# Softmax-weighted rows of a graph attention layer: the fold on VectorE replaced by sums on TensorE, with the numerators in PSUM

## What is computed

```python
feat = einsum('ni,rhid->rnhd', layernorm(x), conv)          # per edge type
el, er = sum(feat[type, src] * attn_l[type]), sum(feat[type, dst] * attn_r[type])
e = leaky_relu(el + er, 0.2)                                 # per edge and head
ex = exp(e - segment_max(e, dst)[dst])
h = segment_sum(ex / segment_sum(ex)[dst] * feat[type, src], dst) + h_bias
x = x + h
x = x + sum_e cw[:, e] * (gelu(layernorm(x) @ W1[e] + b1[e]) @ W2[e] + b2[e])   # cw: two largest of softmax
```

## Time and profile before

| | |
|---|---|
| device time, median of 3 runs | 2616.04 us (2614.4 to 2618.78) |
| span of the profiled execution | 2256.0 us |
| busy: PE, PEld | 1390.8, 1112.0 us |
| busy: DVE, ACT, POOL | 1210.3, 643.8, 1504.5 us |
| mean granted TensorE clock | 0.81 |
| L873 gathers | 1014, mean 1277 ns |
| L1020 multiplies, L1025 adds | 256.1 us (136), 246.2 us (106) |
| L1452 sums | 480 records, 112.1 us |

### The profile page before, as it was taken

One profiled execution on the slowest core, in us unless ns is written; L12 is line 12 of the kernel. 1 busy time (PEld: TensorE's weight loads), 2 busy tenths in 40 slices (PEclk: granted clock), 3 DMA queues, 4 the chain that ended last, 5 costly groups with the idle time before them and its releaser, 6 DMA issues.

```text
span 2256.0 us, 26567 instructions
## 1 busy us (share of the span) xinstructions
PE 1390.8 (62%) x7174; PEld 1112.0 (49%) x7174; DVE 1210.3 (54%) x2282; ACT 643.8 (29%) x2351; POOL 1504.5 (67%) x1213
## 2 busy tenths in 40 slices
PE   2637994016877766676766676656666455465456
PEld 1313441006767665666656565555565354465344
DVE  5413004146767656655656565665666454567462
ACT  3212331013443333333333232332333321223121
POOL 1604113388888888878888888888888887888530
PEclk9878997557999888888887878788888777786677
DMA  5462333743333333333333333333333333323210
GB/s 152 155 161 75 128 134 136 208 123 88 86 83 81 90 88 90 88 90 87 87 92 82 90 85 86 84 85 87 86 86 84 92 89 97 85 80 82 67 37 3
DMA packets 113692, 214.93 MB, mean 95 GB/s; under 512 B 58478, under 2 KB 70357, under 8 KB 109510
## 3 DMA queue, kind: packets, MB, share of 16 engines
q0 software_dynamic: 57936, 153.93, 25.8%
q1 hardware_dynamic: 38688, 25.68, 4.3%
q10 hardware_dynamic: 16892, 33.82, 4.0%
HBM read 172.86 MB, written 44.87 MB: 97 GB/s over the span
## 4 chain that ended last, share of the span: by engine, by line
POOL 56%; issue 17%; PE 3%; POOLq 2%; DVE 2%; ACT 0%; DMA 0%; DVEq 0%; ACTq 0%; SPq 0%
POOL rows L873 52%; PE y_ps L1436 1%; POOL node_row L890 1%; POOL out_dram L881 1%; PE hid_ps L1422 1%; POOL xrows L873 1%; POOLq L886 1%; POOLq L921 1%; POOLq L792 0%; DVE xrows L1084 0%; DVE xrows L1088 0%; DMA xrows<-table,idx_x 0%; ACT hT L1332 0%; POOLq L909 0%; DVE xo L1177 0%
## 5 line engine op out<-in xcount | busy, mean ns | idle before, releaser
L873 POOL DMA_INDIRECT rows<-table,idx_st x1014 | 1294.8, 1277 | 309.0 <-issue 308.7
L1436 PE MATMUL y_ps<-w,hT 128*128 128x256 f32 (+1 forms) x1920 | 526.6, 432 | 530.5 <-ACT hT L1332 514.4
L1436 PEld LDWEIGHTS y_ps<-w,hT 128*128 128x128 f32 (+1 forms) x1920 | 401.3, 216 | 624.3 <-ACT hT L1332 545.6
L1422 PE MATMUL hid_ps<-zT,w 128*128 128x128 f32 (+1 forms) x3840 | 486.8, 287 | 0.0
L1422 PEld LDWEIGHTS hid_ps<-zT,w 128*128 128x128 f32 x3840 | 472.9, 202 | 17.5 <-ACT hT L1332 11.2
L1332 ACT ACTIVATE hT<-hid_ps,b1t 128x128 f32<-128x128 f32 (+1 forms) x960 | 268.6, 370 | 251.7 <-PE hid_ps L1422 249.4
L1025 DVE TENSOR_TENSOR rows<-rows 128x2080 f32<-128x2080 f32 x106 | 246.2, 2322 | 20.4 <-ACT rows L1342 14.6
L1020 DVE TENSOR_TENSOR rows<-rows,ex 128x2080 f32<-128x2080 f32 (+1 forms) x136 | 256.1, 1902 | 1.6
L983 DVE TENSOR_TENSOR score<-score,rows 128x160 f32<-128x160 f32 x30 | 9.7, 325 | 457.5 <-SPq L838 395.9
L586 PE MATMUL feat_ps<-wc,xnT 128*125 128x512 f32 x480 | 230.7, 627 | 37.2 <-ACT xnT L519 25.1
L1311 ACT ACTIVATE th<-e_diff 128x160 f32<-128x160 f32 x30 | 10.1, 336 | 735.9 <-DVE e_diff L1001 735.9
(11 more groups left out here) (172 smaller groups left out, 974.5 us busy)
## 6 DMA issues: line engine op xcount, KB each, us to landing
table<-stage ACTq DMA_DIRECT2D x30, 1031.2 KB
rows<-table,idx_st POOLq DMA_INDIRECT x1014, 2.8
w<-in_L_ffn_W_dram SPq DMA_DIRECT2D x16, 512.0 KB, 14.3
blocks<-edge_row SPq DMA_DIRECT2D x1, 4351.5 KB, 54.2
x_all<-in_x_dram SPq DMA_DIRECT2D x3, 1250.0 KB
node_tab<-x_all SPq DMA_DIRECT2D x3, 1250.0 KB
wc<-_L_gnn_conv_weights_dram ACTq DMA_DIRECT2D x16, 128.0 KB, 6.7
attnb<-in_L_gnn_attn_l_dram SPq DMA_DIRECT2D x1, 1024.0 KB, 10.8
```

The lines of the kernel that those rows point to most:

```text
L873: q.indirect_dma_start(buf[:, k, :], None, table, bass.IndirectOffsetOnAxis(idx[:, col + k:col + k + 1], 0)).then_inc(landed, 16)
L1422: last = t.matmul(hid_ps[e % 2][:, m * P:m * P + n], w1[:, e, k, m * P:(m + 1) * P], zT[:, k, 0:n], start=(k == 0), stop=(k == KD - 1))
L1436: last = t.matmul(y_ps[p % 2][0:n, (e % 2) * D:(e % 2 + 1) * D], hT[e % 2][:, k, 0:n], w2[:, e, k, :], start=(k == 0), stop=(k == KH - 1))
```

## The change

The numerators are written a second time, into a PSUM bank `dve_ps` that only VectorE uses (`ex_ps`), and VectorE's multiplies read them there; `er9` moves to the same bank. ScalarE still reads them from SBUF. VectorE multiplies slots 0 to 20 (8 and then 13 in one instruction) and, where the degree is over 32, 32 to 39; ScalarE has slots 21 to 31 (44 activations in parts of 16, 16 and 12 where there were 12, 8 and 8). All folds are gone. TensorE adds all slots, 32 or 40, through the identity into `agg_ps`: slots 0 to 20 when VectorE is done (`weighed`), the last 8 under an If on a register that it loads from SBUF, and 21 to 31 when ScalarE is done. It frees the four slot groups one by one for GpSimd (`freed`), which now takes them in the order 0, 1, 2, 3.

```diff
-    BY_ACT = 7
+    ACT_LO, ACT_HI = 21, 32
-    er9 = [sb(f"er9{i}", [P, H, R1]) for i in range(2)]
+    agg_ps, dve_ps = bank("agg_ps"), bank("dve_ps")
+    ex_ps = dve_ps[:, 0:H * NS].rearrange("p (h k) -> p h k", h=H)
+    er9 = [dve_ps[:, H * (NS + i * R1):H * (NS + (i + 1) * R1)].rearrange("p (h r) -> p h r", h=H) for i in range(2)]
...
-            for n, s in enumerate((1, 3, 2, 0)):
+            for s in range(PAIRED):
                 if not isinstance(w, int) or w >= 2:
-                    if s:
-                        pool.wait_ge(folded, (w - 2) * 3 + (n + 1))
-                    else:
-                        pool.wait_ge(agg_ok, w - 1)
+                    pool.wait_ge(freed, (w - 2) * PAIRED + (s + 1))
...
             st.did(v.tensor_scalar(ex[:], rden[:], 2.0, -1.0, ALU.mult, ALU.add))
+            st.did(v.tensor_scalar(ex_ps, rden[:], 2.0, -1.0, ALU.mult, ALU.add))
...
-        def weighted(par, s, skip=0):
-            lo, hi = s * SLOTS + skip, (s + 1) * SLOTS
+        def weighted(par, lo, hi):
             r = rows[par][:, lo:hi, 0:AGG].rearrange("p k (h c) -> p k h c", h=H)
-            return v.tensor_tensor(r, r, bc(ex[:, :, lo:hi].rearrange("p h k -> p k h"), 3, HC), ALU.mult)
+            return v.tensor_tensor(r, r, bc(ex_ps[:, :, lo:hi].rearrange("p h k -> p k h"), 3, HC), ALU.mult)
...
-            st.did(weighted(par, 0))
+            st.did(weighted(par, 0, SLOTS))
...
-            st.did(weighted(par, 1))
+            st.did(weighted(par, SLOTS, ACT_LO))
...
             with dve.If(degree > PAIRED * SLOTS):
-                weighted(par, PAIRED)
+                weighted(par, PAIRED * SLOTS, NS)
                 dve.drain()
-                fold(par, 0, PAIRED)
-                dve.drain()
-            fold(par, 0, 1).then_inc(folded, 1)
+            st.wait()
+            dve.sem_inc(weighed, 1)
             for _ in gate:
                 pass
-            st.did(weighted(par, 2))
-            st.did(weighted(par, 3, BY_ACT))
-            st.wait()
-            dve.wait_ge(act_weighed, w + 1)
-            fold(par, 2, 3).then_inc(folded, 1)
             between()
-            dve.wait_ge(folded, w * 3 + 2)
-            fold(par, 0, 2).then_inc(folded, 1)
...
-            dve.wait_ge(agg_ok, w + 1)
+            dve.wait_ge(freed, (w + 1) * PAIRED)
...
-                weigh(w, par, 0, 3)
+                weigh(w, par, 21, 25)
                 gelu(u, 2)
-                weigh(w, par, 3, 5)
+                weigh(w, par, 25, 29)
                 gelu(u, 3)
-                weigh(w, par, 5, BY_ACT)
+                weigh(w, par, 29, ACT_HI)
...
-            pe.wait_ge(folded, w * 3 + 3)
-            for k in range(SLOTS):
-                last = t.matmul(agg_ps[:, 0:AGG], ident[:], rows[par][:, k, 0:AGG], start=(k == 0),
-                                stop=(k == SLOTS - 1))
-            last.then_inc(agg_ok, 1)
+            def add(k, start=False, stop=False):
+                return t.matmul(agg_ps[:, 0:AGG], ident[:], rows[par][:, k, 0:AGG], start=start, stop=stop)
+
+            degree = pe.value_load(nb_row[0:1, bass.ds(w * 2 + 1, 1)], min_val=0, max_val=E)
+            after(pe, acc_ok, w)
+            pe.wait_ge(weighed, w + 1)
+            for k in range(ACT_LO):
+                last = add(k, start=(k == 0))
+                if k % SLOTS == SLOTS - 1:
+                    last.then_inc(freed, 1)
+            with pe.If(degree > PAIRED * SLOTS):
+                for k in range(PAIRED * SLOTS, NS):
+                    add(k)
+            pe.wait_ge(act_weighed, w + 1)
+            for k in range(ACT_LO, ACT_HI):
+                last = add(k, stop=(k == ACT_HI - 1))
+                if k % SLOTS == SLOTS - 1:
+                    last.then_inc(freed, 1)
```

More of the change, by code:

```diff
@@ L642, in phase2 @@
     assert PAIRED == 4 and STATIC == 5 and W % 2 == 0
-    N_FRONT, N_EX, N_BEGIN, N_POST, N_GATE, N_MIX = 6, 6, 5, 16, 11, 1 + NE
+    N_FRONT, N_EX, N_BEGIN, N_POST, N_GATE, N_MIX = 6, 5, 5, 16, 11, 1 + NE
     N_XFRONT, N_XEX, N_CHUNK = 7, 7, 25
@@ L735, in phase2 @@
     act_weighed = sem("act_weighed")
-    folded = sem("folded")
-    agg_ok = sem("agg_ok")
+    weighed = sem("weighed")
+    freed = sem("freed")
     acc_ok = sem("acc_ok")
@@ L864, in _ @@
         q = nc.gpsimd
-        for i in range(2):
-            q.memset(er9[i][:], MASKED).then_inc(const_ok, 1)
         bt = Batches(pool, "pool")
@@ L977, in scores @@
             st.wait()
-            st.did(v.tensor_tensor(eh, bc(er9[par][:], 1, n), bc(hot, 2, H), ALU.mult))
+            st.did(v.tensor_tensor(eh, bc(er9[par], 1, n), bc(hot, 2, H), ALU.mult))
             st.wait()
@@ L1012, in exps @@
             st.did(v.tensor_scalar(ex[:], rden[:], 2.0, -1.0, ALU.mult, ALU.add))
+            st.did(v.tensor_scalar(ex_ps, rden[:], 2.0, -1.0, ALU.mult, ALU.add))
             st.wait()
             return st
-        def weighted(par, s, skip=0):
-            lo, hi = s * SLOTS + skip, (s + 1) * SLOTS
+        def weighted(par, lo, hi):
             r = rows[par][:, lo:hi, 0:AGG].rearrange("p k (h c) -> p k h c", h=H)
-            return v.tensor_tensor(r, r, bc(ex[:, :, lo:hi].rearrange("p h k -> p k h"), 3, HC), ALU.mult)
-        def fold(par, s, t):
-            a, b = (rows[par][:, i * SLOTS:(i + 1) * SLOTS, 0:AGG] for i in (s, t))
-            return v.tensor_tensor(a, a, b, ALU.add)
+            return v.tensor_tensor(r, r, bc(ex_ps[:, :, lo:hi].rearrange("p h k -> p k h"), 3, HC), ALU.mult)
         def weigh_all(w, par, st, gate, between):
-            st.did(weighted(par, 0))
+            st.did(weighted(par, 0, SLOTS))
             for _ in range(2):
                 next(gate, None)
-            st.did(weighted(par, 1))
+            st.did(weighted(par, SLOTS, ACT_LO))
             degree = dve.value_load(nb_row[0:1, bass.ds(w * 2 + 1, 1)], min_val=0, max_val=E)
@@ L1036, in weigh_all @@
                 next(gate, None)
+            with dve.If(degree > PAIRED * SLOTS):
+                weighted(par, PAIRED * SLOTS, NS)
+                dve.drain()
             st.wait()
-            alone(dve, dve_passed)
-            with dve.If(degree > PAIRED * SLOTS):
-                weighted(par, PAIRED)
-                dve.drain()
-                fold(par, 0, PAIRED)
-                dve.drain()
-            fold(par, 0, 1).then_inc(folded, 1)
+            dve.sem_inc(weighed, 1)
             for _ in gate:
                 pass
-            st.did(weighted(par, 2))
-            st.did(weighted(par, 3, BY_ACT))
-            st.wait()
-            dve.wait_ge(act_weighed, w + 1)
-            fold(par, 2, 3).then_inc(folded, 1)
             between()
-            dve.wait_ge(folded, w * 3 + 2)
-            fold(par, 0, 2).then_inc(folded, 1)
-            assert st.n == N_EX
+            assert st.n == N_EX, st.n
         def take(w):
-            dve.wait_ge(agg_ok, w + 1)
+            dve.wait_ge(freed, (w + 1) * PAIRED)
             v.tensor_copy(acc[:], agg_ps[:, 0:AGG].rearrange("p (h c) -> p h c", h=H)).then_inc(acc_ok, 1)
@@ L1267, in _ @@
         dve.sem_inc(cleared, 1)
+        for i in range(2):
+            v.memset(er9[i], MASKED).then_inc(const_ok, 1)
         dve.wait_ge(const_ok, 2)
@@ L1335, in weigh @@
         def weigh(w, par, lo, hi):
-            if lo == 0:
+            if lo == ACT_LO:
                 act.wait_ge(ex_step, w * N_EX + 2)
-            for k in range((PAIRED - 1) * SLOTS + lo, (PAIRED - 1) * SLOTS + hi):
+            for k in range(lo, hi):
                 for h in range(H):
@@ L1342, in weigh @@
                     last = a.activation(r, r, ACT.Copy, scale=ex[:, h, k:k + 1])
-            if hi == BY_ACT:
+            if hi == ACT_HI:
                 last.then_inc(act_weighed, 1)
@@ L1366, in window @@
             else:
-                weigh(w, par, 0, BY_ACT)
+                weigh(w, par, ACT_LO, ACT_HI)
             nb, g = bt.enter(w)
```

2 lines of the change are left out of this document (1 added, 1 removed).

## The result

The changed kernel takes 3117.75 us (3098.07 to 3126.99), before 2615.6 in the same comparison: a ratio of 1.190, 95% interval 1.186 to 1.195. It is 19% slower, where I had forecast 3% faster.

The account below looks back on a forecast made before the run. GpSimd's gathers, stalled by VectorE, were taken as the bound, moving to TensorE. Savings of 155 us less 78 for clock and queue gave net -77: 2616 to 2539 us, range 2455 to 2605.

Parts of the forecast that it names:

- the median of 2616.04 lies 360.0 above it, and I leave that part as it is: Starting point of the sum: profiled span 2256.0 us, with the 360.0 us up to the median carried over unchanged.
- The bound moves to TensorE: TensorE's round, 48.7 us for 32 slots and 52.4 for 40, bounds almost every window instead of GpSimd.
- GpSimd's waits: Gathers for the window after next start 3.7 us into TensorE's sums, taking slot groups as they are freed.
- Covered.: Gathers end after 43.3 us (28) or 58.4 (40), before they are wanted at 63.4 or 70.8.
- The stalls go: GpSimd's gathers beside VectorE's two-SBUF-input instructions lose their stalls, 11 to 12 us a window; mean near 0.95 us.
- ScalarE's part: Sixteen more activations put off gelu 3 by 1.92 us; TensorE waits 2.56 there, its first piece grows to 26.7.
- The clock: TensorE's clock falls after the 2.56 us wait in two of three windows: 4.0 us each, 2.7 a window.
- The queue: Register load, If and added waits in TensorE's queue cost 0.3 us a window.
- The rival for slower: TensorE's register load and If drain its queue and lower the clock: 9.6 us a window, 2711 us; chance 0.14.
- stalls stay: Rival: VectorE instructions with a PSUM input still stall GpSimd's gathers; +39, 2578 us; chance 0.09.

Follow-up runs that it names:

- the kernels in which gathers and multiplies do meet: Changed kernel with eleven memsets a gather, 2387.8 us (1.054); kernel before with PSUM numerators, one drain a window, three memsets a gather, 2254.77 us (0.997).
- the run with 1.70 us beside the folds and 0.95 beside the multiplies: Kernel before with multiplies reading numerators in PSUM, folds kept in SBUF, one drain a window and three memsets a gather: 2254.77 us, ratio 0.997.
- its control on the kernel before: Kernel before with one drain a window alone, no memsets: 2597.38 us, ratio 0.992.

## Why the prediction was wrong, point by point

**"the median of 2616.04 lies 360.0 above it, and I leave that part as it is".** This is the step that failed: with it the waits for late reports, 42% of the changed kernel's chain, stayed out of the sum. Whether the sign would have come out right where reports are prompt is open. The timed executions have spans as long as their times (2616.4 against 2618.08), and the 360 us lie inside the windows, as waits for late reports. The whole sum was made for prompt reports, a regime in which the timed kernels don't run. A difference of 14% between a profile and its times was a finding to be explained, not a constant to be carried over. The section ahead of the prediction says that it lies outside the span, which no row showed.

**"The bound moves to TensorE", with rounds of 48.7 and 52.4 us.** Right in its terms for 32 slots, wrong as a round. Sums: 14.19 us for 32 slots, forecast 14.7. z to sums: 26.8, forecast 26.7. But in the timed runs the round holds the run of gathers too, in series, so 84.7. Where reports were prompt it was 50.35.

**"GpSimd's waits" ... "Covered."** Wrong. GpSimd waits 655.6 us for TensorE's sums in 37 places; in the kernel before it waited 202.0 for VectorE's folds, in places of 13.7 us at most. My account of it: late reports delay the sums, sums delay the gathers, gathers delay the reports. The change ties the start of the gathers to the sums, which stand right ahead of TensorE's last exchange with ScalarE in the window. This place in the order is how I explain that the change loses so much more than the kernel before. It was argued from the timelines; no run moved the gathers' start alone.

**The stalls go:** right, but the mean of 951 ns for 1277 doesn't show it by itself. Only 8 of the 1014 gathers of the changed kernel run beside a multiply of the rows, since they start after the sums; that the mean came out as forecast is in part luck. What shows it are the kernels in which gathers and multiplies do meet: 0.95 us beside a multiply with its numerators in PSUM, in 159 and 184 gathers, where the kernel before had 2.63. Against the unchanged kernel in the regime of its times (1122 ns) less is gained, and with GpSimd off the path it is worth little: 1% from the numerators alone in the kernel before. With spaced gathers and GpSimd as bound it is worth 101 us. These rows refute the rival "stalls stay". The inference of the Trainium skill's page "SBUF — State Buffer", section "Who interferes with whom", that a product of two inputs in SBUF doesn't hold up the making of descriptors, doesn't agree: in the run with 1.70 us beside the folds and 0.95 beside the multiplies, what differs is the second input's place.

**ScalarE's part:** right to 0.02 to 0.3 us; in the windows shown the wait before expert 3's second products was 2.82 us and, where reports are prompt, 2.54; forecast 2.56. **The clock** after it: I took a fall in two of three windows. In the changed kernel the first fifteen hidden products behind it start within 1.56 us at the full clock, and over 2.2 us in only four of 29 windows. At the forecast's 4.0 us each that is 16 us in place of 70, so the term was too large by some 55 us. **The queue:** 0.3 us a window forecast, nothing measured (ratios 1.189 with load and If left out against 1.190, and 1.000 with them added to before).

**The rival for slower** had the right sign and a mechanism that costs nothing here. What the runs showed, TensorE's reports late during a run of gathers, was in none of my rivals. The measured time is 513 us above the range of 2455 to 2605.

**What is shown, and what is not.** Shown: memsets between the gathers bring the reports through (ScalarE's 1237 us of remote waits before its gelus become 997 with three memsets, 426 with eight and 1.41 us between starts, and 4.6 with sixteen), and it is not the bytes or the If; nor is it the one drain a window, by its control on the kernel before. The number of sums is 138 us of the 500. The best version on a chip with late reports is the kernel before with three memsets (0.939) or, with eight, with the numerators in PSUM (0.951), on different chips and so not ranked. The changed kernel never got below the kernel before: 1.190, 1.170, 1.002, 1.004 with 0, 3, 8, 16 memsets, and 1.054 with eleven on the prompt chip. Open: what in a gather holds the reports up, its signals or its descriptors, was not told apart, nor why only TensorE's are late, nor whether recording the trace takes part. Why three memsets help the kernel before at all, with 1.27 us from gather to gather for 1.25, is open; the threshold may lie there, or another instruction between two gathers may matter in itself. Whether the prompt reports belong to that one chip of four, and why, is open too. And the changed kernel without memsets was not run on that chip. An estimate for it: the eleven memsets lengthen GpSimd's 40 gathers by 40 x 0.24 = 9.6 us and the drain adds some 3 us a window in a kernel whose chain is GpSimd's by 58%; without them it could come below 2264 us, as forecast, but nothing shows it.

## What to carry to other kernels

Before a sum is made, the profiled execution must be reconciled with the times: if they differ by more than the spread of the times, a second profile is worth more than any term. A mean that comes out as forecast isn't yet the mechanism: count how many instructions met the condition at all. Where one engine issues a long unbroken run of indirect gathers, look for "remote" in the waits for TensorE and for starts that follow the end of the run by a few microseconds; then a little room between the gathers can be worth more than a faster gather. And a cure that is right about one engine pays only while that engine is the bound.

## What the runs showed of the hardware

In the changed kernel a report from TensorE to ScalarE came up to 35 us late while GpSimd issued gathers 1.25 us apart, in 25 of 28 windows 4.1 to 6.6 us after the last of them; with 1.41 us it mostly came between the gathers, and with 1.64 us nearly at once (4.6 us of ScalarE's remote waits in the windows). VectorE's recorded reports in the same runs of gathers were on time. Halving each row's bytes didn't change it. Of four chips three ran the same kernel in 2583 to 2621 us (one of them in 2621 and, in a later comparison, in 2583) and one in 2264; within a comparison its runs agree within 1%. A gather takes 0.95 us beside a multiply with one input in PSUM, and 2.63 beside the same with both in SBUF. A drain behind a gather on GpSimd costs 2.4 us, one ahead of a window's gathers some 3.1 us (idle time before the node-row gather, line 890 and then 891, went from 101.8 to 192.0 us over 29 windows). A one-column memset on GpSimd takes 0.04 us in a row of eight.
